# Layer 1's attention: its first transfers begun a stage earlier, and a lead-in that prepares one group of four

## The reference

```python
x = x + _L0_ffn_ref(_layernorm(x, axis=-1), ...)         # the mixture in front, 8 x 256 tokens of 128
x = x + _L1_xattn_ref(_layernorm(x, axis=-1), ctx_1024, ctx_1024, ...)
# _L1_xattn_ref: q = query @ Wq + bq, k = ctx @ Wk + bk, v = ctx @ Wv + bv, in 16 heads of 8,
#   softmax(q k^T / sqrt(8)) v for 256 queries and 1601 keys per batch, 8 batches, then @ Wo + bo
```

## Time and profile before

| | |
|---|---|
| time, median of 3 runs | 4446.2 us (4436.0 to 4447.31) |
| the profiled execution's own time | 4450.81 us |
| its span, first to last instruction | 4449.0 us |
| PE busy | 92% of the span |
| DVE busy, ACT busy | 62%, 63% |
| mean granted TensorE clock | 0.955 of full speed |

### The profile page before, as it was taken

How to read it: one execution, slowest core, us unless ns; L and a number is a source line. 1 busy time by engine, 2 the same in 40 slices (tenths; PEclk the granted TensorE clock), 3 DMA queues, 4 the chain that set the end, 5 groups by cost and what they waited for, 6 DMA issues and landing times. The chain is left out here.

```text
span 4449.0 us, 76944 instructions
## 1 busy us (share of the span) xinstructions
PE 4107.6 (92%) x26955; PEld 2939.0 (66%) x26988; DVE 2775.4 (62%) x6291; ACT 2799.3 (63%) x4880; POOL 821.4 (18%) x727
## 2 busy tenths in 40 slices
PE   7897999999889999999999999779999999988799
PEld 6654454454467777777777777537888888865467
DVE  7655887788455656556565655465555555548556
ACT  6523676667357666666666667427777777756457
POOL 2100000000000000000000000005777777751100
PEclk9898899999899999999999999889999999989899
DMA  2101433221100000000000000010000000000000
GB/s 72 38 1 31 75 46 46 38 42 21 43 12 1 12 12 1 13 1 12 1 13 1 12 1 1 14 36 16 8 8 8 7 3 1 1 9 1 28 14 8
DMA packets 79712, 79.33 MB, mean 18 GB/s; under 512 B 10372, under 2 KB 72996, under 8 KB 78220
## 3 DMA queue, kind: packets, MB, share of 16 engines
q1 hardware_dynamic: 74140, 67.95, 7.3%
q10 hardware_dynamic: 5184, 6.32, 0.4%
HBM read 51.31 MB, written 4.19 MB: 12 GB/s over the span
## 5 line engine op out<-in xcount | busy, mean ns | idle before, releaser
L2415 POOL TENSOR_TENSOR L3a_p_lo<-L3a_wq,L3a_p_hi 128x512 fp32r<-128x512 f32 (+1 forms) x480 | 616.5, 1294 | 268.6 <-ACT L3a_p_hi L2365 262.7
L1283 DVE CUSTOM_DVE_ANT_0 L2a_sc<-L2a_score,L2a_mask_n 128x804 f32<-128x804 f32 x512 | 499.1, 992 | 107.0 <-issue 80.2
L1186 ACT ACTIVATE L2a_pt<-L2a_ring 128x512 f32<-128x512 f32 x768 | 430.9, 598 | 185.7 <-PE L2a_ring L1072 184.1
L621 ACT ACTIVATE L1a_work<-L1a_ring 128x1024 f32<-128x1024 f32 x416 | 412.4, 1026 | 174.0 <-PE L1a_ring L439 172.7
L742 DVE TENSOR_REDUCE L1a_mx<-L1a_ring 128x2 f32<-128x1024 f32 x384 | 456.9, 1222 | 65.8 <-PE L1a_ring L458 61.8
L1072 PE MATMUL L2a_ring<-L2a_ident,L2a_sc 128*128 128x128 f32 x3072 | 439.4, 281 | 5.7 <-ACT L2a_sc L1171 1.9
L1171 ACT ACTIVATE L2a_sc<-L2a_sc,L2a_nb 128x1608 f32<-128x1608 f32 x256 | 417.3, 1632 | 0.7 <-DVE L2a_nb L1288 0.7
L2503 DVE TENSOR_REDUCE L3a_mx<-L3a_ring 128x1 f32<-128x402 f32 (+2 forms) x640 | 316.5, 538 | 144.9 <-PE L3a_ring L2217 137.2
L1072 PEld LDWEIGHTS L2a_ring<-L2a_ident,L2a_sc 128*128 128x128 f32 x3072 | 345.5, 143 | 80.6 <-issue 43.2
L2364 ACT ACTIVATE L3a_wq<-L3a_ring 128x512 f32<-128x512 f32 (+1 forms) x480 | 283.5, 591 | 158.9 <-PE L3a_ring L2139 103.3
L1087 PE MATMUL L2a_res<-L2a_pt,L2a_v 128*64 128x256 f32 (+1 forms) x3328 | 373.4, 381 | 1.6 <-ACT L2a_pt L1186 1.6
(11 more groups left out here) (749 smaller groups left out, 9085.1 us busy)
## 6 DMA issues: line engine op xcount, KB each, us to landing
L1a_keys<-L1a_k_hi SPq DMA_DIRECT2D x224, 52.0 KB
L1a_cx<-in_ctx SPq DMA_DIRECT2D x8, 768.0 KB
L2a_cx<-in_ctx SPq DMA_DIRECT2D x8, 768.0 KB
L1a_keys<-L1a_k_lo SPq DMA_DIRECT2D x112, 52.0 KB
L0a_cx<-in_ctx SPq DMA_DIRECT2D x16, 320.0 KB, 3.6
L3a_cx<-in_ctx SPq DMA_DIRECT2D x16, 320.0 KB, 3.8
L2a_mask_u<-in_mask SPq DMA_DIRECT2D x16, 200.1 KB, 4.4
L1a_scr_q<-L1a_keys SPq DMA_DIRECT2D x3, 1024.0 KB
```

The lines of the kernel that those rows point to most:

```text
L621: act.activation(probs[:, (par * NU + u) % c.PS, :, :], ring[tile][:, :, :], ACT.Exp).then_inc(tile_free[tile], 1)
L1186: ins = act.activation(pt[:, t:t + 4, g // 3, q], bank[:, :].rearrange("p (t q) -> p t q", t=4), ACT.Copy)
L1283: dve.tensor_tensor_reduce(sc[:, two, e, w].rearrange("p (k j) -> p k j", k=2), score[e][:, :, 0:CH], mask_n[:, r % 2, w].rearrange("p (k ...
L2415: pool.tensor_tensor(p_lo[0:r, at % PL, 0:W], probs[0:r, at % 2, 0:W], p_hi[0:r, at % PH, 0:W].bitcast(F32), ALU.subtract).then_inc(part_o ...
```

## The change

`HeadsAhead` owns the weights' tiles and the context tile. When L0f is the phase in front, SP issues there, behind the mixture's own `w2`, the context of batch 0 (without its tail of 65 rows) and all 15 weights. In the lead-in only group 0's keys, the first quarter of x and `own(0)` remain. The 14 other steps (`rest`) each stand behind one of the 14 `tops` of group 0: k_hi/k_lo of batch 0 (4), `own` of groups 1 to 3, the other quarters of x (3), the queries of the later batches (4). All use the one bank `res`, each after the step before it. The keys of groups 1 to 3 of batch 0 are no longer merged by DVE but copied by SP as for the later batches (36 transfers of 52 KB), with their constants (four transfers). The inverse roots move to POOL (`rsqrt_chunk`, with `pow`), as do three quarters of the norm. DVE clears only the part of `v` that is not written later.

```diff
+        tops = [n for kind, off, n in self.order if kind == "tops" and n[0] == 0]
+        self.rest = [("high", k) for k in range(self.KB)] + [("own", g) for g in range(1, self.NG)]
+        self.rest += [("turn_x", k) for k in range(1, 4)] + [("query", k) for k in range(4)]
+        self.beside = dict(zip(tops, self.rest))
...
+class HeadsAhead:
...
+    def begin(self, sp):
+        self.context(sp, 0, self.c_first)
+        for tile, dram in self.loads:
+            sp.dma_start(tile[:], dram).then_inc(self.w_in, 16)
...
             sp.wait_ge(zero_ok, 1)
-            load_context(0)
-            for tile, dram in loads[0::2]:
-                sp.dma_start(tile[:], dram).then_inc(w_in, 16)
+            load_tail(0)
             sp.wait_ge(pre_full, KB)
             load_context(1)
-            sp.wait_ge(ql_ok, QC)
+            sp.wait_ge(keys_ok, KB)
+            for r in range(4):
+                at = slice(32 * r + 3 * c.DH, 32 * r + 32)
+                sp.dma_start(keys[at, 0, 1:NG, :].bitcast(F32),
+                             keys[at, 0, 0:1, :].bitcast(F32).broadcast_to([c.DH, NG - 1, JP])).then_inc(const_first, 16)
+            sp.wait_ge(rest_free, rest_at("high", KB - 1) + 1)
+            for g in range(1, NG):
+                replicate_keys(g, 0)
+            sp.wait_ge(rest_free, len(c.rest))
             for copy, rows in enumerate((q_hi, q_hi, q_lo)):
                 sp.dma_start(scr_q[:, copy].rearrange("r d g j -> r (d g) j"), rows.bitcast(F32)).then_inc(q_put, 16)
             sp.wait_ge(q_put, 48)
             sp.wait_ge(blank_ok, 1)
             for r in range(4):
                 at = slice(32 * r + 3 * c.DH, 32 * r + 32)
-                sp.dma_start(keys[at, 1, :, :].bitcast(F32), keys[at, 0, :, :].bitcast(F32)).then_inc(const_in, 16)
+                sp.dma_start(keys[at, 1, :, :].bitcast(F32),
+                             keys[at, 0, 0:1, :].bitcast(F32).broadcast_to([c.DH, NG, JP])).then_inc(const_in, 16)
...
             for k in range(KB):
                 first_key(0, k)
-            pe.wait_ge(xn_ok, 1)
-            for k in range(QC):
-                first_turn_x(k)
-            for g in range(1, NG):
-                for k in range(KB):
-                    first_key(g, k)
...
+            pe.wait_ge(xn_ok, 1)
+            turn_x(claim_first("turn_x", 0), 0, pre_full)
+            pe.wait_ge(const_ok, 1)
+            pe.wait_ge(pre_free, first_at("turn_x", 0) + 1)
+            own(claim_first("own", 0), 0, pre_full)
+            pe.wait_ge(pre_free, len(first))
+            pe.wait_ge(keys_ok, KB)
...
+                if i == 0 and isinstance(b, int) and b == 0:
+                    pe.wait_ge(queries_ok, g + 1)
+                    if g == 1:
+                        pe.wait_ge(const_first, 64)
+                elif i == 0 and g == 0:
...
+                if i == 0 and g:
+                    pe.wait_ge(k_in[g], b * 192 + 192)
...
                 mm.then_inc(tile_full[tile], 1)
+                if isinstance(b, int) and b == 0 and n in c.beside:
+                    rest(*c.beside[n])
...
-            dve.memset(v[:, :, :, :], 0.0)
+            dve.memset(v[:, :, :, c.H * c.VE:c.VW], 0.0)
...
+            stats_chunk(dve, x, st, range(4)).then_inc(mv_ok, 1)
...
+            dve.wait_ge(rs_ok, 1)
+            dve.drain()
+            norm_chunk(dve, xn, x, st, range(4)).then_inc(xn_ok, 1)
```

More of the change, by code:

```diff
@@ L292, in build_heads @@
         piece = lambda i: (i // 6, i // 3 % 2, i % 3) if i < 12 else (i - 12, None, 3)
-        first = [("turn_c", k) for k in range(KB)] + [("key", (0, k)) for k in range(KB)] + [("turn_x", k) for k in range(QC)]
-        first += [("key", (g, k)) for g in range(1, NG) for k in range(KB)] + [("own", g) for g in range(NG)]
-        first += [("query", k) for k in range(QC)]
+        first = [("turn_c", k) for k in range(KB)] + [("key", (0, k)) for k in range(KB)] + [("turn_x", 0), ("own", 0)]
         first_at = lambda kind, n: first.index((kind, n))
+        rest_at = lambda kind, n: c.rest.index((kind, n))
+        highs = [s for s in c.rest if s[0] in ("high", "query")]
         first_bank = lambda kind, n: bank_of(first_at(kind, n) % (2 * c.RING))
@@ L312, in replicate @@
                 for g in range(NG):
[L313 to L317, removed]
+                    replicate_keys(g, par)
             def prepare(n, par, more=True):
@@ L473, in values @@
                     else:
[L474 removed]
+                        pe.wait_ge(rest_free, len(c.rest))
                 for jt in tiles:
@@ L553, in _ @@
         def _(act):
-            for tile, dram in loads[1::2]:
-                act.dma_start(tile[:], dram).then_inc(w_in, 16)
             def first_full(kind, n):
@@ L584, in first_own, with tops @@
                                          scale=cols[:, 3 + 2 * e:4 + 2 * e])
-                ins.then_inc(pre_free, 1)
-            def first_query(k):
-                bank = first_full("query", k)
-                act.activation(q_hi[:, k * 512:(k + 1) * 512], bank, ACT.Identity, bias=bq[:, 0:1], scale=1.0).then_inc(qh_ok, 1)
-            act.wait_ge(w_in, 16 * len(loads))
+                ins.then_inc(signal, 1)
+            def tops(b, par, n):
+                if not (isinstance(b, int) and b == 0 and n in c.beside):
+                    return
+                kind, k = c.beside[n]
+                act.wait_ge(rest_full, rest_at(kind, k) + 1)
+                if kind == "high":
+                    w = span_of(k)
+                    act.activation(k_hi[:, w], res[:, 0:w.stop - w.start], ACT.Identity, bias=bk[:, 0:1],
+                                   scale=1.0).then_inc(rest_high, 1)
+                elif kind == "own":
+                    own(res, k, rest_free)
+                elif kind == "turn_x":
+                    turn_x(res[:, :], k, rest_free)
+                else:
+                    act.activation(q_hi[:, k * 512:(k + 1) * 512], res[:, :], ACT.Identity, bias=bq[:, 0:1],
+                                   scale=1.0).then_inc(rest_high, 1)
+            act.wait_ge(w_in, W_ALL)
             for k in range(KB):
@@ L655, in project @@
                 act.activation(ft[:, :], aux[:, 0:S], ACT.Identity, bias=bfin[:, 0:1], scale=1.0).then_inc(aux_free, 1)
-            run_bodies(act, c.order, dict(scores=scores, result=result, turn_c=turn_c, key=key, value=value, project=project))
+            run_bodies(act, c.order, dict(tops=tops, scores=scores, result=result, turn_c=turn_c, key=key, value=value, project=project))
         @block.gpsimd
         def _(pool):
+            pool.memset(half[:, :], -0.5)
             pool.memset(one[:, :], 1.0)
+            pool.drain()
+            for n, (t0, t1) in enumerate(((0, 4), (4, NT))):
+                pool.wait_ge(mv_ok, n + 1)
+                rsqrt_chunk(pool, st, half, slice(t0, t1)).then_inc(rs_ok, 1)
+            pool.drain()
+            for k in range(1, QC):
+                norm_chunk(pool, xn, x, st, range(4 * k, 4 * k + 4)).then_inc(xp_ok, 1)
             pool.memset(queries[:, 1, :, :, :].bitcast(F32), 0.0).then_inc(blank_ok, 1)
```

193 lines of the change are left out of this document (109 added, 84 removed).

## The result

The kernel after takes **4454.65 us** (median of 10 runs, 4443.68 to 4461.73) against 4445.78 us of the kernel before (10 runs): ratio **1.0022**, 95% interval 1.0013 to 1.0032. Run once more beside the later experiments it gave 1.0019 (1.0009 to 1.0029). By the 0.3% of the prediction that is no change; both intervals lie above 1, so it is a small loss: 8.9 and 7.1 us by the medians, 6 to 14 us by the first interval. The profiled execution took 4458.35 us, its span 4456.5.

What follows compares the result with a forecast made beforehand. The prediction took lead-in waits, then DVE's maxima, as bounds, with SP's queue before batch 1 taking back the win: 2.2 us later start plus 2.7 restart, +4.9, gives 4451.1 us, range 4434.8 to 4462.6.

Steps and rivals of the forecast that it cites:

- Lead-in: Layer 1's start up to the first maximum: shortened, first maximum at 406.3, 32 us earlier.
- Steps beside the maxima: Steps moved into DVE's stretch of group 0's maxima: end at 442, group 1's third maximum at 445, 13.2 to 19.6 us won.
- the full-clock end: Steps beside the maxima with PE at full clock: group 1's third maximum at 439 instead of 445.
- SP's chain: SP's in-order queue before batch 1: 36 key copies precede the queries' transfer, so group 0's keys are ready at 517.4.
- the 1.5 us of queueing: Queries' transfer to DRAM on SP: 1.5 us added for queueing behind the last key copies, ending at 487.3.
- constants, context and queries: SP's list before batch 1's first key copy: 16.6 us, priced as 14.6 by bytes plus 2 for queueing.
- the prediction's lower end of 9: Low case for constants, context and queries on SP: 9 us, with twice as many engines at work.
- PE's wait: PE before batch 1's first tops: one wait of 15 to 22 us for keys, batch 1 starting 2.2 us later than before.
- Restart: PE after its wait: work resumes at half clock and loses 2.7 us; 0 to 4 possible.
- Mixture in front: Phase before layer 1, where SP starts 1.8 MB early: costs zero, at most 6.4 us.
- Sum: Whole kernel: 2.2 us later start of batch 1 plus 2.7 restart, +4.9 us, giving 4451.1 us.
- the win that stays: Rival, SP's chain ready before 502: 13.2 to 19.6 us stay, time 4427 to 4433; chance 12 in 100.

Runs made afterwards that it cites:

- e3: Kernel after, with batch 1's constants copied group by group, each in front of that group's keys: 4447.78 us, ratio 1.0009 to the kernel before.
- e7: Kernel after, queries staged behind group 0's place, constants group by group, context 2 and group 0's keys before the wait for the queries' transfer: 4444.36 us, ratio 0.9999 to before.
- e8: Kernel after, with the layer's first transfers issued at the layer's own start, as in the kernel before: 4464.03 us, ratio 1.0044 to before.
- e4: Kernel before, with only the early issue of layer 1's context and weights (HeadsAhead) added: 4442.89 us, ratio 1.0000 to before.
- e1: Kernel after, with the queries' three transfers to DRAM issued from ACT's queue instead of SP's: 4455.32 us, ratio 1.0032 to before.
- e9: e7 with the constants of groups 2 and 3 issued behind all key copies: 4433.21 us, ratio 0.9978 to the kernel before.
- e5: Kernel after, with the edits of e1, e2 and e3 together: 4449.3 us, ratio 1.0009 to the kernel before.
- e2: Kernel after, with SP loading batch 2's context before it waits for the queries' transfer to DRAM: 4459.6 us, ratio 1.0039 to before.

## Why the prediction was right

The time (4454.65 against 4451.1) was right, and for the predicted reason: the front is shortened, SP's queue in front of batch 1 gives it back. e3 and e7 show it: with that queue shortened, or group 0 taken out of it, the wait shrinks or goes and the front's win reaches batch 1. Step by step:

- **Lead-in.** First maximum 406.3 forecast, 406.44 measured. e8 adds what the sum took for granted, that the data is there: it is worth 6.2 us.
- **Steps beside the maxima.** The first copy came at 417.34 (418), the last step's merge ended at 444.6 (442), group 1's third maximum at 447.54 (445). So 11.0 us were won and not 13.2 to 19.6. (The 13.2 is a slip: 445 from 458.6 is 13.6.) The two stretches to that mark ran at 0.69 and 0.70 of the clock, so the full-clock end was never in play.
- **SP's chain.** The forecast 418, 451.0, 487.3, 503.9, 517.4 stands against 417.34, 449.98, 484.24, 506.18, 521.25. Terms: copies 32.6 (33.0); queries 34.3 (36.3: the 1.5 us of queueing did not come); **constants, context and queries 21.9 (16.6)**; group 0's copies to PE's start 15.1 (13.5). The third is the term that was mis-sized, by 5.3 us: I had priced the constants, in four rows of 6.6 KB instead of one of 26.6, like 16 key copies, and 2 us for what queues behind. They were slower: the constants moved 48 GB/s (row from 485), batch 0's key copies 57 (418 to 449), and the context behind them held SP for 9 us. Before took 22.1 for the same list. (The rate of the key copies by the earlier trace rows is 0.912 us and not 0.915, which changes little.) In the row from 485 the engines are 0.48 busy, about half of the 16. The Trainium skill's rule ("DMA: Bandwidth & Descriptors", why a DMA increments its semaphore by 16), that the count of engines follows from the slowest dimensions, agrees with that row; the prediction's lower end of 9, with twice as many engines, does not.
- **PE's wait.** 15 to 22 forecast, 17.7 measured; its end 6.1 us later than before instead of 2.2. That the wait itself fits is partly luck: the keys came 3.9 us later than forecast, and PE asked at 503.6, 1.6 us behind the latest time forecast. PE's wait list from 380 to 500 us has no wait for a transfer, so the copies of batch 0's other groups were in time.
- **Restart.** 2.7 forecast. The mechanism held: from PE's start (+6.1) to the mark b1 g0 (544.83 against 536.39, +8.4) it cost 2.3, with the clock at 0.50 from 521.3 to 525.5. The warning of the Trainium skill ("TensorE: Matmul & The Clock Gate", HAM oscillation) holds here at that price.
- **Mixture in front.** 0 forecast; e4, which has the same early transfers and nothing else, gives 1.0000.
- **Sum.** +4.9 forecast; 8.4 at b1 g0, 8.9 and 7.1 by the medians. The shift did not stay one amount, as the prediction had it: it is 10.6 at the last mark, with the half-clock stretches between.

Of the rivals, the win that stays was put down to copies running beside the queries' way. No run shows whether they could: in e1 the queries left no earlier, and in e7 the copies stood behind the context, whose issue held SP until the way was nearly done; the copies without the context in front were not tried. It took another address (e7) and another order (e9) to let the win stay. That a later batch would wait once the first wait was gone, I had excluded for the kernel after (rightly); for e3, e5 and e7 I had not thought of it, and it decided each of them.

Not settled: why e1's and e2's medians stand 5 to 10 us higher over before than that of after does, while their marks are level with it (the kernel before was 3.5 us faster in their set than in the later ones, which may be part of it). That e9's marks lose 4 of 13 us between batch 1 and the end goes with half clock: from b1 g1 on, e9 has 48 us at 0.50 and before 34, and between marks where the two have the same clock they agree within some 0.2 us. Which kernel or execution gets more of them, and why, is open.

## What to carry to other kernels

Before a prologue is shortened, follow the slowest serial chain that starts in it (here one queue's copies, a round trip through DRAM, constants) to the first consumer that has no slack left: if the chain's end does not move, the gain is at most that slack, 9.5 us here. This change also moved the chain's start 14.7 us later (449.98 against 435.30), and so lost even that. A chain is cut by changing what stands in front of the first consumer's part: place the staged data where it doesn't block it, and send what is needed last at the end. And look at marks along the work, not at one wait: a wait can shrink because its engine is late (e1), and what is won can be lost at the next reader of the same queue (e7).

## What the runs showed of the hardware that was not expected

- Issuing a DMA on SP's queue took 21.94 us (e2), 22.44 us (e7) and 22.37 us (e9) for one small transfer while the 3 MB of the queries, issued by SP too, were under way (21.33 us in e7 again), and still 12.07 us in e5, where the queries had gone from ACT's; the same instruction takes 0.56 us later in the kernel. While it hung, SP could issue nothing else.
- The constants' copies from four narrow rows kept the engines 0.48 busy and moved 48 GB/s (after, 485 to 493), from one wide row 0.56 and 53 GB/s (before, 471 to 479); the queries' way to DRAM ran at 0.25 and 106 GB/s (row from 455). The transfer with half the share of engines moved twice the bytes.
- Three DMA issues on ACT cost it 3.83 us and put its table's load of 1.28 us behind them: together they put ACT's first exponential 5.1 us later (e1, counted from the layer's start).
